# First attention stage: the last value projection moved into the group's own first tile, and the turn of the fourth tile behind a projection

## What is computed

```
x = x + attn_a(layernorm(x))     # 16 heads of 16, windows of 32 tokens
x = x + ffn(layernorm(x))        # 16 experts, top 1, capacity 1024
x = x + attn_b(layernorm(x))     # 16 heads of 16, all 1024 tokens, with output weights
x = x + ffn(layernorm(x))
```

```
qkv = layernorm(x) @ w_qkv.T + b_qkv          # 256 -> 768
out1 = attention(q[:32], k[:32], v[:32])      # of each 64 tokens: the first half,
out2 = attention(q[32:], k[32:], v[32:])      # and the second half (rolled, and rolled back)
attention: softmax(q k.T / 4) v               # a head, a window of 32 tokens
```

## Time and profile before

| | us |
|---|---|
| median of 3 timed runs | 6285.84 |
| lowest and highest of them | 6283.96, 6301.84 |
| the profiled execution's own time | 6231.95 |
| its span, from the first to the last instruction | 6230.3 |
| first stage: the last matmul of its values (L511) starts at | 759.3 |

### The profile page before, as it was taken

One profiled execution on the slowest core, in us unless ns is written; L12 is line 12 of the kernel. 1 busy time (PEld: TensorE's weight loads), 2 busy tenths in 40 slices (PEclk: granted clock), 3 DMA queues, 4 the chain that ended last, 5 costly groups with the idle time before them and its releaser, 6 DMA issues. The chain is left out here.

```text
span 6230.3 us, 130514 instructions
## 1 busy us (share of the span) xinstructions
PE 5595.4 (90%) x49152; PEld 3883.2 (62%) x49152; DVE 4544.8 (73%) x7725; ACT 3522.8 (57%) x5185; POOL 1598.4 (26%) x2157
## 2 busy tenths in 40 slices
PE   7888756799997969999999999999999996699998
PEld 5666556699996744444444445444544545689998
DVE  6888656456555658888888888888888874555554
ACT  5666522233333437777777777777777773233332
POOL 5666524333330000111111111111111113533332
PEclk9999955899998979999999999999999996599999
DMA  1111199222226961111111111111111114422221
GB/s 48 47 47 47 51 150 159 88 85 84 95 68 221 352 224 48 58 61 61 62 61 62 61 61 61 61 61 61 61 61 62 61 47 76 61 87 99 82 83 61
DMA packets 434097, 527.85 MB, mean 85 GB/s; under 512 B 52214, under 2 KB 351892, under 8 KB 433712
## 3 DMA queue, kind: packets, MB, share of 16 engines
q1 hardware_dynamic: 400944, 457.71, 26.2%
q0 software_dynamic: 32768, 64.84, 3.4%
HBM read 337.81 MB, written 185.07 MB: 84 GB/s over the span
## 5 line engine op out<-in xcount | busy, mean ns | idle before, releaser
L1642 DVE TENSOR_REDUCE at_best<-at_psM 128x2 f32<-128x1024 f32 x2048 | 2410.7, 1220 | 366.7 <-PE at_psM L1685 366.2
L1598 ACT ACTIVATE at_p<-at_psE 128x1024 f32<-128x1024 f32 (+1 forms) x2688 | 2067.4, 819 | 600.7 <-PE at_psE L1701 567.3
L1701 PE MATMUL at_psE<-at_q,at_k 50*128 50x512 f32 x4096 | 1124.5, 428 | 84.9 <-ACT at_p L1598 83.3
L1685 PE MATMUL at_psM<-at_k,at_q 48*128 48x512 f32 x4096 | 1096.8, 454 | 52.2 <-DMA at_v<-scratch_v 31.3
L1711 PE MATMUL at_psO<-at_p,at_v 128*32 128x256 f32 x16384 | 1098.5, 386 | 0.0
L1701 PEld LDWEIGHTS at_psE<-at_q,at_k 50*128 50x128 f32 x4096 | 560.2, 185 | 482.8 <-ACT at_p L1598 225.7
L1020 ACT ACTIVATE e_h_hi<-e_psH 128x512 fp32r<-128x512 f32 x512 | 305.8, 597 | 913.1 <-PE e_psH L90 913.1
L1095 DVE SCALAR_TENSOR_TENSOR e_h_lo<-e_psH,e_h_hi 128x512 fp32r<-128x512 f32 x512 | 354.4, 692 | 589.2 <-ACT e_h_hi L1020 589.2
L1711 PEld LDWEIGHTS at_psO<-at_p,at_v 128*32 128x32 f32 x16384 | 428.0, 109 | 533.3 <-issue 311.0
L1685 PEld LDWEIGHTS at_psM<-at_k,at_q 48*128 48x128 f32 x4096 | 493.0, 187 | 361.4 <-DVE at_best L1642 172.1
L90 PE MATMUL e_psE<-e_w_hi,e_h_hi 128*128 128x256 f32 x2048 | 582.4, 284 | 0.0
(11 more groups left out here) (185 smaller groups left out, 8715.8 us busy)
## 6 DMA issues: line engine op xcount, KB each, us to landing
e_w_raw<-in_w SPq DMA_DIRECT2D x64, 1024.0 KB
scratch_qk<-cp_qkh SPq DMA_DIRECT2D x64, 512.0 KB
scratch_qk<-cp_qkl SPq DMA_DIRECT2D x64, 512.0 KB
scratch_v<-cp_va SPq DMA_DIRECT2D x32, 1024.0 KB
at_q<-scratch_qk SPq DMA_DIRECT2D x256, 128.0 KB
at_k<-scratch_qk SPq DMA_DIRECT2D x256, 128.0 KB
at_v<-scratch_v SPq DMA_DIRECT2D x128, 256.0 KB
a_x<-in_x SPq DMA_DIRECT2D x32, 512.0 KB
```

The source lines that it names most:

```text
L1598: nc.scalar.activation(P[:, u:u + n, :], src, ACT.Exp, scale=HD ** -0.5).then_inc(p_ready, 1)
L1642: nc.vector.reduce_max(best[j % 2][:, h, :, qt], psM[h][:], AX_X).then_inc(m_taken, 1)
L1685: last = nc.tensor.matmul(psM[h][:, a, :], Q[j][r, 128 * qt:128 * qt + 128], K[j][r, 512 * h:512 * h + 512], start=True, stop=True)
L1701: last = nc.tensor.matmul(psE[:, u - u0 if n == 2 else 2, :], K[j][r, 128 * kc:128 * kc + 128], Q[j][r, 512 * half:512 * half + 512], star ...
```

## The change

Two things move in PE's order, and ACT's order follows them. The projection of the values of a group's fourth tile (part 7) leaves the fourth tile of the group before and goes into the group's own first tile, between the scores and the transposes. And in the fourth tile, projection 5 goes ahead of the turn. The wait of `values` for the whole group's copies becomes a wait of each tile for its own copy. Group 0 still has all its eight projections made ahead of the loop. The last group has no successor and so no transposes behind its projection 7.

```
-        PARTS = [(0,), (1, 2), (3, 4), (5, 6, 7)]
+        PARTS = [(0,), (1, 2), (3, 4), (5, 6)]
...
@@ ACT, group @@
+                    if t == 0 and not (isinstance(g, int) and g == 0):
+                        take(g, s, 7)
                     if t == 0 and ahead:
                         split_hi(g + 1)
                     if t == 3:
-                        takes(5, 6)
+                        takes(5)
                     exps(n, t % 2)
...
                     if t == 3:
-                        takes(7)
+                        takes(6)
...
@@ PE, values @@
-                if t == 0:
-                    pe.wait_ge(proj_taken, 8 * g + 8)
+                pe.wait_ge(proj_taken, 8 * g + 5 + t)
                 pe.wait_ge(pt_ready, 4 * n + 4)
...
@@ PE, group @@
                     if t < 3:
                         scores(g, s, t + 1)
+                    if t == 0 and not (isinstance(g, int) and g == 0):
+                        project(g, 7)
                     if t == 0 and not last_ones(g, 1):
                         transposes(g + 1, 1 - s)
+                    if t == 3 and not last_ones(g, 1):
+                        project(g + 1, 5)
                     if not (isinstance(g, int) and n < 2):
                         turn(n - 2, t % 2)
                     if t > 0 and not last_ones(g, 1):
-                        for part in PARTS[t]:
+                        for part in PARTS[t][t == 3:]:
                             project(g + 1, part)
```

## The result

| | before | changed |
|---|---|---|
| median of 6 timed runs, us | 6285.52 | 6319.21 |
| lowest and highest, us | 6283.95, 6301.86 | 6311.67, 6327.28 |
| ratio to before, 95% interval | | 1.0046 [1.0030, 1.0062] |
| the profiled execution, us | 6231.95 | 6327.28 |
| last start of xhi (the first is at 21.6 in both), us | 718.4 | 754.1 |

The changed kernel is slower by 0.46%, 29 us (19 to 39); that is the distance of the averages, the medians are 33.7 us apart. The two profiled executions differ by 95 us, of which only 35.7 lie in the stage that was changed.

A forecast was written before the change was run, and what follows sets the result against it. A 22.38 us round through DVE, POOL, PE and ACT was taken to bound the kernel. Only projection 7 cost: 30 x 0.85 = 25.5 us on 6285.84 gave 6311.3, range 6300 to 6324, with some 8 us for the medians.

The forecast's parts named there:

- The round: Loop of xlo, DVE's work to a_o, POOL, third tile's values, scores, transposes, xhi: 22.38 us, insertions paid in full.
- Projection 5 ahead of the turn: Fourth tile: its 0.72 us fits PE's 1.04 us wait for oT, the turn keeps its time; worth 0.
- the wait ahead of the third tile's values: PE waiting there for POOL's pt copy: grows from 0.38 to about 1.8 us, taking up both moves' gain.
- Projection 7: First tile, between scores and transposes: delays xhi and xlo by 0.85 us, 30 times, 25.5 us.
- change-over: PE's switch around a piece of projections: 0.20 us paid once a piece, on top of the matmuls' 0.72.
- ACT's copy and the added waits: Copy to VA ahead of xhi hidden by the transposes, per-tile waits met early: 0; copy at worst 11 us.
- PE waits for xlo ahead of projection 0: Behind the fourth tile's values: xlo ends about 0.85 us later, so PE loses another 0.4 us there.
- The clock: Granted clock in the loop: PE busy 19.9 of 23.25 us, 0.86, so expected to stay at 1.00.
- the rival: Clock falls: values to transposes at half clock every round, 3.75 us, 30 times, 112 us, 6424; chance 0.03.
- The sum: Whole kernel: timed median 6285.84 plus 25.5 gives 6311.3 us.
- the bounds of 21.6 to 29.7: Cost of the moved projection in the first tile: 30 x 0.72 to 30 x 0.99 us.
- The rule on the most contended engine: PE as bound: filling its hole before the turn gains 31 x 0.72 = 22.3 us, 6263.5; chance 0.10.

The follow-up runs named there:

- e2: Against the kernel before, only projection 7 moved, to between the first tile's scores and transposes; projection 5 stays behind the turn: 6307.2 us, ratio 1.0035.
- e3: Against the kernel before, projection 5 ahead of the turn and projection 7 behind the next group's scores, in PE's hole: 6280.6 us, ratio 0.9995.
- e5: The changed kernel with projection 7 made twice in a row between scores and transposes: 6325.2 us, ratio to before 1.0063.
- e1: Against the kernel before, only projection 5 moved ahead of the turn in the fourth tile: 6289.6 us, ratio 1.0004.
- e4: The changed kernel with the next group's first scores made twice, as useless work in PE's hole: 6305.8 us, ratio to before 1.0030.
- f1: The kernel before with POOL's inverse deviation (var_eps, rstd) moved ahead of the first tile's bias: 6275.7 us, ratio 0.9981.
- f4: The kernel before with transposes and xhi early, in the fourth tile, projection 5 ahead of the turn, POOL's inverse deviation first: 6251.8 us, ratio 0.9954.
- f3: The kernel before with projection 5 ahead of the turn and POOL's inverse deviation ahead of the first tile's bias: 6268.3 us, ratio 0.9972.

## Why the prediction was right, and where not

**The round.** Right. It was read off the timelines, and e2, e3 and e5 show it: the same six matmuls cost 0.74 us behind the wait for POOL, 0 ahead of it, and twice as many cost 1.46.

**Projection 5 ahead of the turn: 0.** Right, by e1 (ratio 1.0004). The time went where the prediction put it, into the wait ahead of the third tile's values: forecast 1.8 us for both moves together, measured 1.78.

**Projection 7: 0.85 us, 30 times, 25.5 us.** The mechanism was right, the size a little high: 0.74 us, and 20.5 us in e2's stage. The term that was too high is the change-over of 0.20 us, of which I charged more than half. From its start to that of the transposes it takes 0.82 (327.54 to 328.36), but xhi starts 1.15 us behind the transposes (328.36 to 329.51) where it was 1.22 (314.09 to 315.31), and a second projection right behind the first costs only its pitch of 0.72 (e5).

**ACT's copy and the added waits: 0.** Right. The copy ends 0.57 us ahead of xhi. e2 has the per-tile waits too and pays only what projection 7 costs, and no wait of PE in the changed kernel names the copies.

**PE waits for xlo ahead of projection 0.** Right: 331.93 is just behind xlo's end at 331.79. The wait is 0.43 us there, as forecast, and 19.7 us in 26 groups, 0.76 on average.

**The clock.** Here the prediction was wrong. "So I expect 1.00" came from comparing the busy share of a whole period with the end of the stage, and the rival had every group or none. The clock fell in 9 groups of 31, for 14.7 us; a fall cost 1.63 us and not the 3.75 of the rival. e4, with the hole half filled, has none of it. The share over a whole period did not tell: PE is busy for 560.5 of 630 us before, for 551.5 in the changed kernel and for 552.2 in e5, which has no fall.

**The sum.** It came out in range partly by luck. The projection was priced 5 us too high and the clock, 15 us, was left out, so the stage lost 35.7 us, outside the bounds of 21.6 to 29.7. The timed difference of 29 us (19 to 39) is too coarse to tell the two apart, and the 8 us that the range allowed for the medians took up the rest: 6319.2 against 6311.3.

**The rule on the most contended engine.** The Trainium skill ("Perfetto Trace Analysis", Optimization Strategy) has one find the gaps of that engine and make what it waits for come sooner. Taken as filling gaps it misled, as e1 shows; taken by its second half, it held: in f1 to f4 POOL's results come sooner, and the time falls.

**The keys beside POOL's copies.** The Trainium skill ("Perfetto Trace Analysis", Optimizing Scalar/DVE Operations) reminds the reader that GPSIMD and DVE share an SBUF read port (GPSIMD is POOL here). The keys' 1.30 and 2.40 us agree with it; no run here isolates the port as the cause.

## What to carry to other kernels

Before work is moved in an engine's order, look for the wait that ends last on it: ahead of that wait, work is free as long as the hole holds it, behind it, every matmul is paid once a round, however many other holes the engine has. A hole that is filled early only moves to the next wait, unless the engine waited for is made faster too. And collecting small holes into one large one can cost the clock: 15 of the 36 us of this stage. When the round has been shortened, read it anew: here it moved from POOL's copies towards DVE's keys, which the copies had slowed.

## What was not expected of the hardware

- The granted clock fell to its lower level behind a hole of 1.78 us that recurred every 23.14 us, in 9 groups of 31 (1.63 us each). With holes of 0.9 and 1.1 us it never fell in the loop (e4, e2), nor with one of 1.76 us that recurred every 23.86 us (e5), nor with one of 1.7 us in every other group (f3).
- With useless matmuls in that hole the clock stayed up, and the stage ended 13.5 us sooner (e4, one profiled execution of each).
- Three DVE multiplications of 128 x 512 by a mask column took 1.30 us beside POOL's small power operation and 2.40 us beside its 32 x 512 copies; one alone took 0.47 and 0.85 us.
